# A cross-attention and FP4 feed-forward kernel on one Trainium2 core: the down weights are quantized at other places, the opening and the drain are put in another order, and the low products wait

## The reference

```python
x = x + xattn(_layernorm(x), ctx, ctx, Wq, bq, Wout, bout)
x = x + ffn(_layernorm(x), w_gate, w_up, w_down)

# xattn: one correlation over all sequences, its 12 or so best shifts, a softmax over them
q, k_, v = ((t @ Wq + bq).transpose(0, 2, 1) for t in (Q, K, V))
corr = real(ifft(fft(q) * conj(fft(k_)))).mean(axis=(0, 1))
W_topk, I_topk = top_k(corr, int(2 * log(512)));  W_topk = softmax(W_topk)
R = sum(w * roll(v, -shift) for w, shift in zip(W_topk, I_topk))    # repeated for 16 heads
return R @ Wout + bout

# ffn: blocks of 16 are put on the FP4 grid, inputs and weights alike
def fp4_linear(x, w): return einsum('bsk,nk->bsn', quant(x), quant(w))
h = silu(fp4_linear(x, w_gate)) * fp4_linear(x, w_up)      # 256 -> 704
return fp4_linear(h, w_down)                               # 704 -> 256
```

## Time and profile before

| what | value |
| --- | --- |
| median of 3 runs | 526.64 us (526.01 to 527.78) |
| the profiled execution's own time | 528.21 us |
| its span, first to last instruction | 526.4 us |
| PE busy, share of the span | 476.7 us, 91% |
| DVE | 456.9 us, 87% |
| ACT | 391.9 us, 74% |
| POOL | 254.2 us, 48% |

### The profile page before, as it was taken

One profiled execution on the slowest core, in us unless ns is written; L12 is line 12 of the kernel. 1 busy time (PEld: TensorE's weight loads), 2 busy tenths in 40 slices (PEclk: granted clock), 3 DMA queues, 4 the chain that ended last, 5 costly groups with the idle time before them and its releaser, 6 DMA issues.

```text
span 526.4 us, 10114 instructions
## 1 busy us (share of the span) xinstructions
PE 476.7 (91%) x3490; PEld 315.4 (60%) x3490; DVE 456.9 (87%) x762; ACT 391.9 (74%) x670; POOL 254.2 (48%) x326
## 2 busy tenths in 40 slices
PE   4599897858699999999999999999999999899957
PEld 4587787723355666666656666666666666466635
DVE  3789967598679999999999999999999999999981
ACT  3267875775978888888888788888888877766661
POOL 3225550256245566665655556666565558333330
PEclk9989997978899999999999999999999999899989
DMA  8988810432055676576675575656666564444636
GB/s 274 346 264 269 277 51 26 86 85 56 1 95 106 134 131 129 120 132 128 143 125 116 121 140 122 130 116 126 141 121 138 117 118 93 97 97 95 133 69 150
DMA packets 164723, 68.68 MB, mean 130 GB/s; under 512 B 129088, under 2 KB 164416, under 8 KB 164672
## 3 DMA queue, kind: packets, MB, share of 16 engines
q1 hardware_dynamic: 164672, 68.03, 57.3%
HBM read 27.38 MB, written 9.18 MB: 69 GB/s over the span
## 4 chain that ended last, share of the span: by engine, by line
issue 34%; POOL 21%; DVE 20%; PE 13%; ACT 5%; DMA 4%; SPq 1%; POOLq 1%; DVEq 1%; ACTq 0%
POOL ctx_sb L466 13%; POOL sl L482 6%; DVE w_q_lo L1144 4%; DVE ctx_sb L1097 3%; DVE y_h L1176 2%; DVE x_t L895 2%; PE ps L724 2%; ACT h_c L536 2%; PE ps L842 2%; ACT h_c L533 2%; PE ps L843 1%; DMA w_raw<-in_L_ffn_w_up_dram 1%; PE ps L704 1%; PE ps L844 1%; PE ps L714 1%
## 5 line engine op out<-in xcount | busy, mean ns | idle before, releaser
L842 PE MATMUL ps<-guT_hi,a_xT 128*128 128x512 f16 (+1 forms) x384 | 141.9, 370 | 14.1 <-DVE hb L1092 7.4
L843 PE MATMUL ps<-guT_lo,a_xT 128*128 128x512 f16 (+1 forms) x384 | 142.1, 370 | 0.0
L844 PE MATMUL ps<-guT_hi,a_xT 128*128 128x512 f16 (+1 forms) x384 | 141.6, 369 | 0.0
L852 PE MATMUL ps<-dT_hi,hqT 128*128 128x256 f16 x704 | 130.5, 274 | 7.6 <-ACT a_xT L594 5.7
L466 POOL TENSOR_TENSOR ctx_sb<-w_q_lo,sl 128x704 f16<-128x704 f16 x62 | 96.2, 1574 | 29.4 <-DVE ctx_sb L1097 29.3
L533 ACT ACTIVATE h_c<-y_h 128x1408 bf16<-128x1408 bf16 (+3 forms) x39 | 47.8, 1226 | 75.9 <-DVE y_h L1176 58.7
L854 PE MATMUL ps<-dT_lo,hqT 128*128 128x256 f16 x384 | 88.4, 275 | 0.0
L517 POOL TENSOR_TENSOR xs<-xs,w_raw 128x512 f32<-128x512 f32 x30 | 36.0, 1200 | 101.1 <-issue 101.1
L852 PEld LDWEIGHTS ps<-dT_hi,hqT 128*128 128x128 f16 x704 | 69.3, 98 | 18.7 <-issue 6.0
L842 PEld LDWEIGHTS ps<-guT_hi,a_xT 128*128 128x128 f16 x384 | 38.1, 99 | 62.5 <-issue 15.7
L844 PEld LDWEIGHTS ps<-guT_hi,a_xT 128*128 128x128 f16 x384 | 38.2, 100 | 40.5 <-issue 3.5
(11 more groups left out here) (161 smaller groups left out, 863.9 us busy)
## 6 DMA issues: line engine op xcount, KB each, us to landing
xs<-in_x_dram SPq DMA_DIRECT2D x16, 512.0 KB, 6.1
ctx_sb<-in_ctx_dram SPq DMA_DIRECT2D x16, 512.0 KB, 5.1
out_dram<-a_xT SPq DMA_DIRECT2D x64, 128.0 KB, 2.0
w_raw<-a_scratch SPq DMA_DIRECT2D x60, 128.5 KB, 2.7
hqT<-ctx_sb SPq DMA_TRANSPOSE x64, 3.8
w_raw<-in_L_ffn_w_down_dram SPq DMA_DIRECT2D x1, 704.0 KB, 6.3
w_raw<-in_L_ffn_w_gate_dram SPq DMA_DIRECT2D x1, 640.0 KB, 5.9
w_raw<-in_L_ffn_w_up_dram SPq DMA_DIRECT2D x1, 640.0 KB, 6.9
```

The costliest lines, as they stand in the source:

```text
L842: pe.matmul(dst, xt[:, c, :], guT[0][:, c, n0:n1], start=(c == 0), stop=False)
L843: pe.matmul(dst, xt[:, c, :], guT[1][:, c, n0:n1], start=False, stop=False)
L844: last = pe.matmul(dst, xt[:, KC + c, :], guT[0][:, c, n0:n1], start=False, stop=(c == KC - 1))
L852: pe.matmul(dst, hqT[:, j % 4, c, :], dT_hi[:, c, :], start=(c == 0), stop=False)
```

## The change

It has these parts.

- **Opening.** SP issues the third group of inputs ahead of the gate and up weights, and the down weights ahead of the last two groups. `W_FIRST` goes from 2 to 3. DVE takes the third group's statistics and the first `evac_qk` ahead of `w_prepare(0)`, and does `w_prepare(1)` at group 14.
- **Low halves.** `w_lo(g)` on POOL waits until DVE has finished the product of segment g + 1. In the loop `low_h` waits until the next pair's `y_h` is written.
- **Down weights.** Their segments are divided right behind the last `evac_qk`, split on ACT ahead of all eight gate and up fills, and finished on DVE behind the choice of the shifts; fills 8 and 9 are transposed behind the attention, with 28 useless matmuls after them in place of 20, and fills 10 to 12 between the first four gate and up tiles, not before tiles 4 to 6. The DVE work of these weights inside the first stages is gone.
- **Drain.** DVE does the low products of pairs 29 and 30 itself. ACT copies down results out ahead of the last splits, `last_y` writes to a place of its own (`z_y`), and `y_h` of pair 30 is divided ahead of the high product of pair 29.

```diff
-W_FIRST = 2
+W_FIRST = 3
...
+        z_y = w_raw[:, 2 * FF:4 * FF]
...
             load_c(1)
+            load_x(2)
+            load_c(2)
...
-            for i in range(2, NQ):
+            for i in range(3, NQ):
+                if i == NQ - 2:
+                    down_v = w_raw[:, 256 * GU_CH:WCOLS].rearrange("p (c n) -> p c n", n=FF)
+                    sp.dma_start(down_v, w_down.rearrange("(c p) n -> p c n", p=P)).then_inc(s["d_loaded"], 16)
                 load_x(i)
                 load_c(i)
...
             def w_lo(g):
                 pool.wait_ge(s["w_hi"], g + 1)
+                if g + 1 < N_GU:
+                    pool.wait_ge(s["w_steps"], finish_at(g + 1) + 3)
...
-                if pair_ok(st - 3) and st <= NP + 1:
+                if pair_ok(st - 3) and st < NP:
+                    pool.wait_ge(s["yh_done"], st - 1)
                     low_h(st - 3)
...
             keep_v(NQ // QT - 1)
-            evacuate_weights(act, range(EARLY))
+            w_split(N_GU)
+            w_split(N_GU + 1)
             act.wait_ge(s["t_steps"], 3)
             act.activation(wexp[:, :], corr[:, 0, 0:P], ACT.Exp, bias=nmx[:, 0:1]).then_inc(s["t_exp"], 1)
-            evacuate_weights(act, range(EARLY, GU_FILLS))
-            w_split(N_GU)
-            w_split(N_GU + 1)
+            evacuate_weights(act, range(GU_FILLS))
+            w_hi(N_GU)
+            w_hi(N_GU + 1)
...
                 elif st == NP:
+                    residual(2 * st - 8)
+                    residual(2 * st - 7)
                     last_split(0)
-                    residual(2 * st - 8)
+                    residual(2 * st - 6)
+                    residual(2 * st - 5)
                     last_split(1)
-                    residual(2 * st - 7)
...
             pe.wait_ge(s["w_ev"], GU_FILLS)
+            pe.wait_ge(s["x1_done"], 2)
+            pe.wait_ge(s["w_lo"], len(SEGS))
+            for f in range(GU_FILLS, GU_FILLS + 2):
+                transpose_weights(f)
             pe.wait_ge(s["id_out"], 1)
-            for _ in range(20):
-                pe.matmul(bank(6)[:, 0:P], ones[:, :], ident[:, :], start=True, stop=True)
+            for _ in range(28):
+                pe.matmul(bank(4)[:, 0:P], ones[:, :], ident[:, :], start=True, stop=True)
...
+            def low_h(p):
+                dve.wait_ge(s["sl"], p + 2 - SC0)
+                times_runs(hq[:, p % 2, :, FF:2 * FF], h_g, sl[:, (p + 1) % 2, 0:2 * RUN_H], RUN_H).then_inc(s["z_lo"], 1)
...
-                    if pair_ok(p):
+                    if pair_ok(p) and st < NP - 1:
                         high_h(p)
...
                     if pair_ok(j):
                         scaling_h(j)
+                    if st == NP - 1:
+                        high_h(p)
+                        low_h(p)
...
-                if st in (-1, 0):
-                    w_finish(N_GU + 1 + st)
```

More of the change, by code:

```diff
@@ L437, in _ @@
             rstd_a(1)
-            for i in range(NQ):
+            for i in range(NQ + 1):
                 if i + 2 < NQ:
                     rstd_a(i + 2)
-                if turn(i - 2) is not None:
-                    w_lo(turn(i - 2))
+                if turn(i - 3) is not None:
+                    w_lo(turn(i - 3))
             pool.wait_ge(s["w_split"], 3 * N_GU)
@@ L449, in _ @@
                                channel_multiplier=1).then_inc(s["pick_set"], 1)
+            w_lo(N_GU)
+            w_lo(N_GU + 1)
             def last_low_scales(t):
@@ L519, in _ @@
                                        ).then_inc(s["x1_done"], 1)
-                if st in (0, 1):
-                    w_lo(N_GU + st)
         @block.scalar
@@ L656, in _ @@
                 j, n = st - 1, st + 2
-                if st in (0, 1):
-                    w_hi(N_GU + st)
-                if st <= 0:
-                    if st < 0:
-                        scale_high(st)
-                        split_x(n)
+                if st < 0:
+                    scale_high(st)
+                    split_x(n)
                     normalise_x(st + 3)
                     square_x(st + 4)
-                    if st == 0:
-                        scale_high(st)
-                        split_x(n)
-                        silu(0)
-                        silu(1)
+                    if st >= -2:
+                        evacuate_weights(act, range(GU_FILLS + 2 + st, GU_FILLS + 3 + st))
+                elif st == 0:
+                    silu(0)
+                    normalise_x(st + 3)
+                    square_x(st + 4)
+                    scale_high(st)
+                    silu(1)
+                    split_x(n)
+                    evacuate_weights(act, range(GU_FILLS + 2, GU_FILLS + 3))
                 elif st < NP:
@@ L674, in _ @@
                     silu(2 * st)
-                    if st == 2:
-                        evacuate_weights(act, range(GU_FILLS + 2, len(FILLS)))
+                    if st == 1:
+                        evacuate_weights(act, range(GU_FILLS + 3, GU_FILLS + 4))
                     normalise_x(st + 3)
@@ L873, in _ @@
                     gate_and_up(2 * n)
-                    if n == 2:
-                        for f in range(GU_FILLS + 2, len(FILLS)):
-                            transpose_weights(f)
+                    if n == 1:
+                        transpose_weights(GU_FILLS + 3)
                     gate_and_up(2 * n + 1)
-                if n == 1:
-                    pe.wait_ge(s["w_lo"], len(SEGS))
-                    for f in range(GU_FILLS, GU_FILLS + 2):
-                        transpose_weights(f)
+                if n < 2:
+                    transpose_weights(GU_FILLS + 2 + 2 * n)
                 if n == 3:
@@ L998, in _ @@
             last.then_inc(s["q_bias"], 1)
+            stats_a(2)
+            evac_qk(0)
             w_prepare(0)
-            for i in range(NQ):
+            for i in range(1, NQ):
                 if i + 2 < NQ:
                     stats_a(i + 2)
-                if i == 0:
-                    w_largest(0, bank(7)[:, 0:P])
-                if i >= 1:
+                if i >= 2:
                     evac_qk(i - 1)
+                if i == W_FIRST - 1:
+                    w_largest(0, bank(6)[:, 3 * P:4 * P])
                 if i == W_FIRST:
@@ L1210, in _ @@
                 j, p, xa, xb = st - 1, st - 2, st + 1, st + 2
-                if st <= 1 and pair_ok(xa):
+                if st <= 0 and pair_ok(xa):
                     offset_x(xa)
@@ L1246, in _ @@
                     last_scale(0)
+                    last_y(0)
                     offset_h(p)
-                    last_y(0)
+                    grid_h(p)
+                    high_h(p)
+                    low_h(p)
                     gate_up(2 * j + 1)
```

78 lines of the change are left out of this document (42 added, 36 removed).

## The result

The changed kernel takes 509.7 us in the median (508.22 to 512.84), the kernel before 527.21 on the same chip: ratio 0.968, 95% interval [0.963, 0.973]. The forecast was 504.2 with a range of 498 to 512. The span of the profiled execution went from 526.4 to 508.0.

| stretch | ends at | before | after | difference | predicted |
| --- | --- | --- | --- | --- | --- |
| opening | start of the last evac_qk's product | 80.97 | 81.85 | +0.9 | -2.0 |
| middle | first gate tile | 30.00 | 31.56 | +1.6 | +0.6 |
| first pairs | pair 2's division | 46.89 | 37.17 | -9.7 | -10.0 |
| even part | gate tile at 436.66, now 429.07 | 278.80 | 278.49 | -0.3 | 0 |
| last pairs | last pair's gate tile | 52.19 | 47.06 | -5.1 | -4.9 |

What follows compares the result with a forecast made beforehand. PE's own matmuls were taken to bound more than half of the time. Opening -2.0, middle +0.6, first pairs -10.0, last pairs -4.9 and drain -6.1 sum to -22.4 us: 504.2 against the median, range 498 to 512.

Steps and rivals of the forecast that it cites:

- the filled gap against the later loads: Opening: work put into DVE's idle gap gains 2.7 us, later weight loads cost 2.0; net -0.7.
- the low halves: Opening: POOL's low halves no longer run beside DVE's product of scales; -1.3 us, between 0 and 3.4 gained.
- The down weights' reduction: Opening: moved to DVE at group 14, into time DVE has free; no cost, about 1.5 us without that cover.
- Middle: Gate and up fills behind the exponential delay PE's late fills and useless matmuls; +0.6 us, from 0 to 1.9.
- Piece (a): First pairs: less idle time ahead of the first gate tile keeps PE's clock up; all 4.6 us of lost work regained.
- rival 2: First gate tile: the clock falls again, 4.6 us come back, 508.8 us; 15 in 100.
- (b): First pairs: PE's 2.40 us wait for hb shrinks as DVE's two down finishes ahead of it go; -1.9 us.
- (c): First pairs: one dT copy instead of two stands near the split of pair 0; -1.1 us.
- Piece (d): First pairs: with the fills at the first four tiles, the step between pairs falls from 14.31 to 11.93; -2.4 us.
- Last pairs: From pair 25, the low product waits until behind the division, DVE needs less than PE; -4.9 us.
- Rival 4: Last pairs: the low product blocks the next division, DVE needs 12.6 us a pair; 506.6 us, 10 in 100.
- Drain: After the last gate and up tile: PE's waits shrink to 1.8 and about 1.0 us; -6.1 us, bounds -8 and -3.

Runs made afterwards that it cites:

- experiment 9: experiment 1 with the old front of the opening: weights loaded ahead of the third group, reduced before its statistics and the first evac_qk; 502.14 us, ratio 0.951.
- experiment 1: The changed kernel with ACT's copy of v one group earlier, ahead of a weight segment's split; 503.4 us, ratio 0.955.
- experiment 6: experiment 1 without the wait of the weights' low halves on POOL; 507.34 us, ratio 0.962.
- experiment 2: The changed kernel without the eight useless matmuls ahead of the product with cT; 507.44 us, ratio 0.964.
- experiment 8: The changed kernel with the last three fills of the down weights back in front of the sixth gate and up tile; 510.36 us, ratio 0.967.
- experiment 3: The changed kernel with POOL's addition of the attention no longer waiting for DVE's division of x; 506.9 us, ratio 0.961.
- experiment 10: experiment 1 with POOL's addition of the attention, from stage 3 on, behind the low product and the next stage's low scales; 500.02 us, ratio 0.947.
- experiment 4: The changed kernel with POOL's low product no longer waiting for the next y_h; 515.5 us, ratio 0.979.
- experiment 5: The kernel before, with only one edit: POOL's low product waits for the next y_h; 520.53 us, ratio 0.986.
- experiment 7: The changed kernel with ACT's copies of the down results back behind the last splits; 516.67 us, ratio 0.978.
- experiment 11: experiment 10 with twelve more useless matmuls while the correlation is out, and 38 instead of 28 ahead of the first gate tile; 499.98 us, ratio 0.946.
- experiment 12: The changed kernel with the edits of experiment 1, experiment 9 and experiment 10 together; 499.65 us, ratio 0.947.

## Why the prediction was right or wrong

The time is 5.5 us above the forecast and inside the range. Of the signs that the prediction named, the idle time ahead of the first gate tile (2.50), the clock above 0.9, the missing waits on dT copies, the even period and the drain's waits came. The earlier last evac_qk did not, pair 2's division is at 150.58 and not at 145 to 148, and one sign of being wrong did come: the first gate tile is 2.44 us later, and the limit was 2.

**Opening: the term was wrong, in its sign.** Its steps were a net -0.7 for the filled gap against the later loads, and -1.3 for the low halves. The first: the weights came 2.1 later as taken (+2.0), but putting the front back made the opening no longer (experiment 9), so a net gain of the new front, with the gap's 2.7 in it, is not to be seen. The second had its size: from the sixth to the twelfth evac_qk, three segments, it is 24.52 us before (44.23 to 68.75) and 23.43 in experiment 1 (41.61 to 65.04), 1.1 less; only the cause is POOL's order, not the wait (experiment 6). The down weights' reduction, costed at nothing, made the last four steps 0.8 longer there (12.22 to 13.00). The step that failed is one that the sum doesn't have: that `W_FIRST` moves the segments to the odd groups, and with them a split and a high half on ACT ahead of its copy of v. I had priced DVE's queue and left out what is queued on ACT. It cost 4.9 us (experiment 1), more than the 2.9 by which the term was off (+0.9 against -2.0), since the same shift also brought the first steps forward.

**Middle: right in kind, too small.** The delay was put at 0.6, from 0 to 1.9, and was 1.6. The upper bound supposed a stretch at half clock more, but there is none: the half clock was there before. What is new is PE's wait of 2.02 for ACT's copies and one more late fill, 0.7 us, against a slack of 0.72. The prediction had the order (fills behind the exponential), but it took its delay from the slack and not from what that order does to PE's wait. Leaving the eight matmuls out does not get the 1.6 back (experiment 2).

**First pairs: the sum was right, two of its steps not.** Piece (a): the clock's 4.6 was to come back whole. From the first gate tile to pair 0's division (at 127.11 before) it was 16.14 and is 13.98; in experiment 1, where the clock stays up, it is 12.63: so the whole is 3.5, of which the fall at 113.2 keeps 1.35. This is rival 2, at a third of its price. Pieces (b) and (c) have to be taken together: from pair 0's division to pair 1's it is 5.2 us less (16.44 to 11.27), where 3.0 was forecast. Not all of that need be theirs: before, the granted clock was 0.50 in the last 2.5 us of this stretch. PE's wait for hb is not gone but has moved on, 0.74 and 3.97. Piece (d) has the right size, 2.4, but not the cause that I gave: with the fills at their old place the step is still 11.99 (experiment 8). Which of the rest makes it (the finishes out of DVE's first stages, the high and low halves out of ACT's and POOL's) was not separated.

**Even part: right, in part by luck.** The wait for y_h passes, as worked out. But I called PE the bound with 11.8 of 11.93, and the edit makes an instruction wait that is part of the real bound. PE needs 11.71, and what holds the period is the ring of DVE and POOL (experiments 3 and 10). The earlier trace rows had its mark: a wait of 0.64 for sl in every pair. The loop was read as a matter of PE's busy share, 278.9 of 282, in which 0.22 us of idle time a pair hides, because the modelled ends overlap the next start.

**Last pairs: right, in size and cause.** -5.1 against -4.9, shown from both sides by experiments 4 and 5. One reading was not right: the division at 446.67 that took 2.05 was not beside the low product, which had ended at 446.46, but beside POOL's next instruction:

```profile
446.43 0.81 POOL L482 TENSOR_TENSOR sl<-bm,sh 128x240 f16<-128x240 f32 x1
```

The low product slowed the two products ahead of the division, from 0.36 and 0.41 to 0.93 and 1.74. With the division's 0.43 that is 2.3 us a pair, the difference between DVE's 13.14 a pair before (446.67 to 459.81) and 10.79 after. Rival 4 did not come: DVE's product behind the division stays at 0.68 beside POOL's low product, and DVE needs those 10.79, where the prediction allowed it 11.3.

**Drain: right in size.** -5.7 against -6.1, with both waits at their forecast size. With ACT's old order all of it is gone, the clock included (experiment 7). Whether ACT's order would do it without the drain's other edits was not run.

By the Trainium skill ("SBUF — State Buffer", section "Who interferes with whom") a DVE instruction with two SBUF inputs and a GpSimd one that reads SBUF exclude each other, and the later one blocks. The trace agrees, and the order decides who pays. With the low product first (experiment 4, 433.66 to 436.95), DVE's product at 435.50 takes 1.73 in place of 0.41. With the division of x first, at 438.72, POOL's low product at 438.88 pays instead, 3.39 in place of 3.00. Rival 4 had the rule and not the order.

## What to carry to other kernels

When a table or a constant moves work to other turns of a loop, list what then stands in front of each short hand-over on every engine that takes part, not only on the one that the edit is about: here a 0.4 us copy behind a split that waits cost 4.9 us. A constant short wait in every round of a loop that looks bound by PE can be a ring; follow it round once, and compare its sum with PE's own work between two starts. And where two engines collide in SBUF, put the instruction that can afford it second: the addition behind the low scales (experiment 10) gave DVE's divisions the whole 0.22 us a pair, dropping its wait (experiment 3) 0.15.

## What was not expected of the hardware

The granted clock did not follow idle time alone. Both levels, 1.00 (2.4 GHz) and 0.50 (1.2 GHz), appear behind the same instructions. With the same 2.50 us of idle time ahead of the first gate tile it was 0.50 there in the changed kernel and 1.00 in experiment 1; in experiment 11 it fell at 89.4 behind idle times of only 0.6, 2.02 and three of under 0.2. The Trainium skill ("TensorE: Matmul & The Clock Gate", section "Part 1: The HAM clock gate") says that where the clock changes differs from run to run. The traces here agree in kind: they are of different kernels, one execution each, with the same instructions up to the fall. In this kernel that is worth up to 3.5 us at a place, as much as several of the edits; and behind the same short wait of 3.9 us (experiments 10 to 12) the low level lasted 7, 3.5 and 0 us.
